# ScalarE's order within a tick: exponentials behind the copies and the side stages

## The chip, the core and the metric

The kernel runs on one core of a Trainium2 chip. The metric is the device time of the whole program in microseconds. It has five engines that matter here: TensorE (PE in the profile; PEld is its weight load), VectorE (DVE), ScalarE (ACT), GpSimd (POOL) and SyncE (SP), which only issues transfers here. Each runs its own list of instructions in order, and they wait for each other by semaphores.

## The reference, cut

Two layers over x of 16 sequences x 256 tokens x 128 features. All is float32.

```python
x  = L0_attn_x
xn = _layernorm(x)
s  = softmax attention of xn, 16 heads of 64, causal, then @ Wo + bo
g  = silu(top-1 routed experts(xn) + shared ffn(xn))
x  = x + s * g
xn = _layernorm(x)
s  = linear attention (elu + 1, cumulative sums, 16 heads of 8)
g  = silu(two transformer layers: l2-normed q and k, rotary,
          local attention with window 64, 8 heads of 64, gated gelu ffn)
x  = x + s * g
```

## The kernel before

The tokens are worked in 8 blocks `b` of 512 (4 tiles of 128 tokens, 2 sequences). The two softmax attentions (kind 0: the causal one of the first layer; kind 1: the local one, two layers `l` per block) are cut in the same way: a *pair* is two heads over both sequences of a block, a *step* is a pair over one sequence (`s` 0 or 1). There are 256 steps.

A plan written by hand (class `Plan`) lays the steps out over 348 *ticks*, at most one step in a tick; some ticks have none. It hangs everything else, the *side stages*, on ticks too: projections `qkv` of one tile of tokens, `lin` (the projections of the linear attention), `cum` (its cumulative sums as matmuls), `wo`, `glu`, `down1`, `v` (the values of kind 0, four banks), `ffn`, the experts `eT`, `eg`, `ed` of ticks 8 to 29, and so on. Every engine walks over the same ticks in its own function and writes its instructions in an order fixed by that function. So the order of an engine's work is the order of the lines in its tick loop, and nothing is moved at run time.

For the step `st` of tick t the work is spread over four ticks:

- TensorE in tick t: `logits` (L541, L544), each head into one of two `s` banks; in tick t+1: `transposes` of the weights `p` (L552), which wait for the exponentials; in tick t+2: `values` (L568, L571), and where s is 1 `merge` (L578), the transposes of the spread sums. Its own order in a tick is: `produce` (q or k of a coming pair, L521 or L531), `logits` of t, `transposes` of t-1, side stages of t, `values` and `merge` of t-2.
- VectorE in tick t: `masked` (L975) adds the mask, scales, takes the maximum; in tick t+1 `copies` of head 0 out of PSUM (L985), `inverse` of the sums (L991); in tick t+3 `scaled` (L996). Then its side stages: for `qkv` these are `mix` (L1158, L1162), `rot` (L1167), `rr` (inverse roots, from L1172) and `kn` (L1258).
- ScalarE in tick t: `exps` (L812, L813), four exponentials that wait for `masked`; in tick t+1 `copies` of head 1 (L826), which wait for `transposes`; in tick t+2 `merge` (L790, rT). `produce` (L790, q or k) evacuates a bank of q or k. Its side stages evacuate the banks that TensorE fills in the same tick: `qkv` five instructions (L889, L890 twice, L790), `lin` (L832, L833), `cum` (L840), `glu` (L911), `phi` (L895), `xT` (L877, L795, L796) and others.

All banks of q, k, merge and most side stages are one ring of two, `mm`. TensorE waits (`mm_bank`) until ScalarE has emptied the bank of two uses before. A `qkv` stage fills three of them, so its third bank waits for the first to be emptied. ScalarE's `raw` and `sq` buffers of a tile are double too, and `qkv` of a tile waits for `rot` of the tile two before (`rot_ready`).

GpSimd spreads the inverse sums (`expand`, L1272), rotates q and k of a tile (L1377, L1378), multiplies in `cum` (L1342) and whitens (L293). Every side stage of it waits for its input by semaphore.

A block has 36 ticks in the steady part. They hold, in this order: a run of four ticks with `qkv` of local layer 0 (ticks 111 to 114 for block 2), whose rotation ends in tick 115 and whose pairs are first produced in tick 116; then twelve `cum` ticks; `glu` of the layer before in tick 125; `glu` of this block in tick 135, in a stretch without steps; four `qkv` ticks of local layer 1 (138 to 141, steps only in the first two). Numbers of ticks below are of this block.

Of the kernel before, what the change touches and what calls it, by code (L numbers as in the profile page):

```python
# [781 lines left out]
def scalar(nc, act, c, plan, mm, s, pt, o):  # L782
# [19 lines left out]
    def produce(which, st):  # L802
        evacuate(c.qk[which][:, st.pair % 4, :], "qk"[which], st.pair)

    def exps(st):
        if st.s == 0 and st.pair >= 2:
            act.wait_ge(c.rden_ready, st.pair - 1)
        for h in range(2):
            u = 2 * st.n + h
            act.wait_ge(c.s_done, s.done("s", st.n, h))  # L810
            den, p = c.den[:, st.pair % 2, 2 * st.s + h, :], c.p[:, u % 4, :]
            A(p[:, 0:P], p[:, 0:P], ACT.Exp, bias=c.nmax[:, u % 4, 0:1], scale=-1.0, accum_out=den[:, 0:1])  # L812
            A(p[:, P:SB], p[:, P:SB], ACT.Exp, bias=c.nmax[:, u % 4, 1:2], scale=-1.0, accum_out=den[:, 1:2])\  # L813
                .then_inc(c.exp_done, 1)

    def merge(pair):
        if pair:
            act.wait_ge(c.o_done, o.done("o", pair - 1))
        evacuate(c.rT[:, :], "m", pair)

    def copies(st):
        u = 2 * st.n + 1
        act.wait_ge(c.pt_full, pt.full("t", st.n, 1))
        if st.n >= 2:
            act.wait_ge(c.pv_done, st.n - 1)
        A(c.pt[:, u % 4, :], c.pt_ps[pt.slot("t", st.n, 1)][:, 0:SB], ACT.Copy).then_inc(c.pt_done_act, 1)  # L826
# [104 lines left out]
    for tick in range(plan.length):  # L931
        for which, st in plan.produce.get(tick, ()):
            produce(which, st)
        if plan.step(tick):
            exps(plan.step(tick))
        if plan.step(tick - 1):
            copies(plan.step(tick - 1))
        if tick == 4:
            act.wait_ge(c.p1_loaded, c.P1_LOADS)
            act.wait_ge(c.hT_zero, 1)  # L940
        for seg in plan.side.get(tick, ()):
            if seg[0] in stage:
                stage[seg[0]](*seg[1:])
        if (st := plan.step(tick - 2)) and st.s == 1:
            merge(st.pair)

# [541 lines left out]
def program(nc, c, w, dram):  # L1488
    with ExitStack() as ctx:
        buffers(nc, ctx, c)  # L1490
        plan = Plan()
        rings = count_units(c, plan)
        c.CONST_LOADS = 16 * 8
        with nc.Block() as block:
            @block.sync
            def _(sp):
                sync(nc, sp, c, plan, *rings, dram, w)

            @block.tensor
            def _(pe):  # L1500
                tensor(nc, pe, c, plan, *rings)

            @block.scalar
            def _(act):
                scalar(nc, act, c, plan, *rings)

            @block.vector
            def _(dve):
                vector(nc, dve, c, plan, *rings)

            @block.gpsimd
            def _(pool):
                gpsimd(nc, pool, c, plan, *rings, dram)
# [81 lines left out]
```

## Time and profile before

| | us |
|---|---|
| median of three runs | 2309.12 (2306.81 to 2309.9) |
| the profiled execution | 2310.23 |
| its span | 2308.4 |
| TensorE busy | 1871.7 (81%) |
| VectorE busy | 1266.9 (55%) |
| ScalarE busy | 1239.2 (54%) |
| GpSimd busy | 805.3 (35%) |
| mean granted TensorE clock | 0.909 of full |

TensorE is the busiest engine and still idle for a fifth of the span, in pieces of 0.3 to 12 us. What the change does is to be read from those pieces: which engine ended them, and in which tick. Around the span lie 1.8 us of the profiled execution.

### The profile page before, as it was taken

To read this page: it belongs to the slowest core of one execution; us is meant where nothing else is said; L and a number is where in the kernel's file an instruction comes from. 1 tells how busy PE (TensorE), PEld (TensorE's weight loads), DVE (VectorE), ACT (ScalarE), POOL (GpSimd) and SP (SyncE) were. 2 spreads that over 40 slices of the span, in tenths; PEclk is the share of its full clock that TensorE was granted. 3 is DMA by queue.
4 is the path that set the end of the run, shared out by engine and by line. 5 is a ranking of instruction groups with operands and counts; after the bars stand their busy time and mean duration, and the time that the engine had idled before them with its cause. 6 is when DMAs were issued, how large, how long until landed. Compare 5 with 4: busy or idle time off the path is not lost.

```text
span 2308.4 us, 34655 instructions
## 1 busy us (share of the span) xinstructions
PE 1871.7 (81%) x10900; PEld 1169.5 (51%) x10900; DVE 1266.9 (55%) x4083; ACT 1239.2 (54%) x3559; POOL 805.3 (35%) x912
## 2 busy tenths in 40 slices
PE   5599987996789878887888779987888778857856
PEld 4377754554455445453555446544546345534534
DVE  4344446555655456546755565545655565466654
ACT  2445545654665546545565465555664566445534
POOL 2732224323432333214532343214432353244431
PEclk9799998997999989998999898988999899979978
DMA  7155400000000000000000000000000000000000
GB/s 226 37 175 168 157 17 8 1 1 6 1 1 14 6 1 1 15 1 1 6 1 15 1 1 1 19 1 1 1 10 6 1 1 1 5 5 1 6 0 5
DMA packets 49711, 53.26 MB, mean 23 GB/s; under 512 B 6386, under 2 KB 42236, under 8 KB 49532
## 3 DMA queue, kind: packets, MB, share of 16 engines
q0 software_dynamic: 7808, 27.79, 3.7%
q1 hardware_dynamic: 41724, 23.26, 3.5%
q8 instruction: 91, 1.49, 0.3%
q14 instruction: 88, 0.72, 0.1%
HBM read 41.60 MB, written 9.44 MB: 22 GB/s over the span
## 4 chain that ended last, share of the span: by engine, by line
PE 56%; DVE 15%; ACT 13%; issue 9%; POOL 6%; DMA 1%; DVEq 0%; SPq 0%; POOLq 0%; ACTq 0%
PE ps L596 5%; PE ps L568 5%; PE ps L552 4%; PE ps L521 4%; PE ps L544 4%; PE ps L541 4%; PE ps L670 3%; ACT p L812 3%; ACT p L813 3%; PE ps L531 3%; PE ps L578 2%; PE ps L512 2%; PE ps L679 2%; PE ps L725 2%; POOL h L293 2%
## 5 line engine op out<-in xcount | busy, mean ns | idle before, releaser
L812 ACT ACTIVATE p<-p,nmax 128x128 f32<-128x128 f32 x512 | 201.7, 394 | 359.8 <-DVE nmax L975 355.8
L975 DVE CUSTOM_DVE_ANT_0 p<-ps,mask,nrq 128x128 f32<-128x128 f32 (+1 forms) x512 | 183.0, 413 | 275.0 <-PE ps L544 275.0
L975 DVE CUSTOM_DVE_ANT_0 p<-ps,mask 128x128 f32<-128x128 f32 (+1 forms) x512 | 152.3, 354 | 263.7 <-PE ps L544 248.8
L670 PE MATMUL ps<-wqkv,hT 128*128 128x512 f32 x384 | 204.6, 643 | 99.3 <-ACT big L890 72.1
L1272 POOL COPY rdx<-rden 128x256 f32<-128x256 f32 x256 | 102.9, 431 | 521.0 <-DVE rden L991 520.1
L813 ACT ACTIVATE p<-p,nmax 128x256 f32<-128x256 f32 x512 | 252.3, 493 | 0.0
L552 PE MATMUL ps<-ident,p 128*128 128x128 f32 x1536 | 243.1, 296 | 5.8 <-ACT pt L826 2.0
L552 PEld LDWEIGHTS ps<-ident,p 128*128 128x128 f32 x1536 | 176.9, 149 | 101.1 <-issue 91.4
L531 PE MATMUL ps<-ident,big 128*128 128x128 f32 x512 | 92.9, 324 | 135.9 <-DVE big L1167 91.9
L1377 POOL TENSOR_TENSOR big<-big,rots 128x512 f32<-128x512 f32 x64 | 100.8, 1575 | 291.9 <-ACT big L890 291.7
L568 PE MATMUL ps<-pt,v 128*64 128x256 f32 x1024 | 178.9, 430 | 0.0
L544 PE MATMUL ps<-k,q 64*128 64x256 f32 x1024 | 170.5, 411 | 0.0
L670 PEld LDWEIGHTS ps<-wqkv,hT 128*128 128x128 f32 x384 | 64.6, 194 | 200.8 <-ACT big L890 124.8
L1342 POOL TENSOR_TENSOR big<-big,qkb 128x360 f32<-128x360 f32 (+1 forms) x96 | 82.4, 858 | 223.4 <-ACT big L840 222.9
L541 PEld LDWEIGHTS ps<-k,q 64*128 64x128 f32 x1024 | 85.1, 201 | 145.0 <-issue 81.0
L541 PE MATMUL ps<-k,q 64*128 64x128 f32 x1024 | 136.7, 346 | 25.5 <-DVE nmax L975 13.3
L985 DVE COPY pt<-ps 128x384 f32<-128x384 f32 x256 | 141.5, 553 | 22.0 <-PE ps L552 21.5
L531 PEld LDWEIGHTS ps<-ident,big 128*128 128x128 f32 x512 | 68.4, 165 | 161.7 <-issue 124.9
L790 ACT ACTIVATE rT<-ps 128x512 f32<-128x512 f32 x128 | 75.9, 593 | 134.9 <-PE ps L578 133.9
L596 PE MATMUL ps<-wo,attT 128*128 128x128 f32 x1024 | 134.8, 295 | 7.9 <-DVE attT L996 6.1
L596 PEld LDWEIGHTS ps<-wo,attT 128*128 128x128 f32 x1024 | 131.2, 210 | 16.6 <-issue 9.7
L790 ACT ACTIVATE q<-ps 128x512 f32<-128x512 f32 x128 | 76.1, 595 | 114.1 <-PE ps L531 76.9
(214 smaller groups left out, 4025.6 us busy)
## 6 DMA issues: line engine op xcount, KB each, us to landing
slots_in<-xn SPq DMA_DIRECT2D x1, 2560.0 KB, 14.0
v<-slots_in SPq DMA_DIRECT2D x20, 128.0 KB
slots_out<-v SPq DMA_DIRECT2D x20, 128.0 KB
big<-in_x SPq DMA_DIRECT2D x4, 512.0 KB, 6.3
x<-in_x SPq DMA_DIRECT2D x8, 256.0 KB, 3.0
out_x<-x SPq DMA_DIRECT2D x8, 256.0 KB, 2.3
wqkv<-in_wqkv SPq DMA_DIRECT2D x2, 768.0 KB
xn<-in_x SPq DMA_DIRECT2D x6, 256.0 KB, 3.3
```

Source lines behind the costliest of these rows:

```text
L531: last = nc.tensor.transpose(bank[:, t * P:(t + 1) * P], c.qkr[:, t, a:a + P], c.ident[:, :])
L541: MM(banks[h][:, 0:P], q[f:f + HD, 0:P], k[f:f + HD, 0:P], start=True, stop=True)
L544: MM(banks[h][:, P:SB], q[f:f + HD, P:SEQ], k[f:f + HD, :], start=True, stop=True).then_inc(c.s_full, 1)
L552: last = nc.tensor.transpose(bank[:, j * P:(j + 1) * P], c.p[:, u % 4, j * P:(j + 1) * P], c.ident[:, :])
L568: MM(bank[f:f + HD, q:q + SEQ], v[:, 2 * st.s, a:a + HD], pts[h][:, 0:SEQ], start=True, stop=False)
L596: last = MM(bank[:, t * P:(t + 1) * P], c.attT[kind][:, i, t * P:(t + 1) * P], w, start=i == 0, stop=i == LAST)
L670: MM(bank[:, :], c.hT[:, t * P:(t + 1) * P], c.wqkv[:, l, i * INNER1:(i + 1) * INNER1], start=True, stop=True).then_inc(c.mm_full, 1)
L790: A(dst, mm_bank(*name)[:, :], ACT.Copy).then_inc(c.mm_done, 1)
L812: A(p[:, 0:P], p[:, 0:P], ACT.Exp, bias=c.nmax[:, u % 4, 0:1], scale=-1.0, accum_out=den[:, 0:1])
L813: A(p[:, P:SB], p[:, P:SB], ACT.Exp, bias=c.nmax[:, u % 4, 1:2], scale=-1.0, accum_out=den[:, 1:2])\
L975: last = V.tensor_tensor_reduce(out=c.p[:, u % 4, a:b], in0=bank[:, a:b], in1=c.mask[st.kind][:, P * (1 - i):SEQ], scale=scale, scalar=3e3 ...
L985: V.tensor_copy(c.pt[:, u % 4, :], bank[:, 0:SB]).then_inc(c.pt_done, 1)
```

## The change

In ScalarE's tick loop the call of `exps` for the step of this tick moves from ahead of `copies` to behind the side stages. It still stands ahead of `merge` of the step two ticks before. No instruction is added or removed, and no other engine's order changes.

```diff
@@ scalar(), tick loop
         for which, st in plan.produce.get(tick, ()):
             produce(which, st)
-        if plan.step(tick):
-            exps(plan.step(tick))
         if plan.step(tick - 1):
             copies(plan.step(tick - 1))
...
         for seg in plan.side.get(tick, ()):
             if seg[0] in stage:
                 stage[seg[0]](*seg[1:])
+        if plan.step(tick):
+            exps(plan.step(tick))
         if (st := plan.step(tick - 2)) and st.s == 1:
             merge(st.pair)
```

ScalarE in a `qkv` tick of local layer 0 (tick 113), from the second head's exponentials or from the copy on. `p` are the weights, `pt` the transposed ones, `mn` belongs to `phi`, `big` holds `sq` and `raw`, `v1` the values of the local attention, ps0 and ps1 are the `mm` ring, ps5 is a bank of the transposes. Before:

```order
L812 ACTIVATE p,den<-p,nmax 128x128
L813 ACTIVATE p,den<-p,nmax 128x256
L826 ACTIVATE pt<-ps5 128x384
L895 ACTIVATE mn<-mn 128x256
L889 ACTIVATE big<-ps1 128x512
L890 ACTIVATE big<-ps1 128x512
L889 ACTIVATE big<-ps0 128x512
L890 ACTIVATE big<-ps0 128x512
L790 ACTIVATE v1<-ps1 128x512
```

and now:

```order
L826 ACTIVATE pt<-ps5 128x384
L895 ACTIVATE mn<-mn 128x256
L889 ACTIVATE big<-ps1 128x512
L890 ACTIVATE big<-ps1 128x512
L889 ACTIVATE big<-ps0 128x512
L890 ACTIVATE big<-ps0 128x512
L790 ACTIVATE v1<-ps1 128x512
L812 ACTIVATE p,den<-p,nmax 128x128
L813 ACTIVATE p,den<-p,nmax 128x256
```

The exponentials now stand behind the evacuation of all three banks of the projection.

ScalarE in the tick with four banks of values of kind 0 (tick 128; `v0` are those values, `big` with ps0 is the bank of a cumulative sum). Before:

```order
L813 ACTIVATE p,den<-p,nmax 128x256
L826 ACTIVATE pt<-ps5 128x384
L840 ACTIVATE big<-ps0 128x360
L790 ACTIVATE v0<-ps1 128x512
L790 ACTIVATE v0<-ps0 128x512
```

and now:

```order
L826 ACTIVATE pt<-ps5 128x384
L840 ACTIVATE big<-ps0 128x360
L790 ACTIVATE v0<-ps1 128x512
L790 ACTIVATE v0<-ps0 128x512
L790 ACTIVATE v0<-ps1 128x512
L790 ACTIVATE v0<-ps0 128x512
L812 ACTIVATE p,den<-p,nmax 128x128
L813 ACTIVATE p,den<-p,nmax 128x256
```

The evacuation of the cumulative sum, on which the second bank of values depends, has left its place behind the exponentials.

ScalarE in a `glu` tick with a step (tick 125; `ff` is the gated buffer). Now:

```order
L826 ACTIVATE pt<-ps5 128x384
L911 ACT_TABLE_LOAD
L911 ACTIVATE ff<-ps1,gb1 114x512
L911 ACTIVATE ff<-ps0,gb1 114x512
L911 ACTIVATE ff<-ps1,gb1 113x512
L840 ACTIVATE big<-ps0 128x360
L812 ACT_TABLE_LOAD
L812 ACTIVATE p,den<-p,nmax 128x128
```

The load of the exponential's table, which stood in the next tick, comes ahead of this tick's exponentials. The number of table loads is 32 in both programs.

## Rows read from the trace of the kernel before

**Rows 1.** Page, part 1: busy us, share of span, instructions.
```profile
PE 1871.7 (81%) x10900; PEld 1169.5 (51%) x10900; DVE 1266.9 (55%) x4083; ACT 1239.2 (54%) x3559; POOL 805.3 (35%) x912
```

**Rows 2.** Waits of TensorE: who, for whom, total us, times, longest us.
```profile
PE ps L531 <- DVE big L1167: 91.9, 15, 11.6
PE ps L506 <- POOL h L293: 78.3, 16, 7.8
PE ps L670 <- ACT big L890: 72.1, 48, 3.1
PE ps L670 <- ACT v L833: 26.8, 16, 3.1
...
PE ps L531 <- ACT v L833: 7.7, 9, 2.4
...
PE ps L521 <- ACT big L840: 6.1, 4, 2.5
PE ps L512 <- ACT big L840: 5.2, 3, 3.0
...
PE ps L552 <- ACT p L813: 1.1, 2, 0.8
```

**Rows 3.** Group by line and shape: count, busy us, mean ns, idle before.
```profile
L812 ACT ACTIVATE p<-p,nmax 128x128 f32<-128x128 f32 x512 | 201.7, 394 | 359.8 <-DVE nmax L975 355.8 <-issue 3.6
```

**Rows 4.** Windows: ticks 111 to 116; us, then busy of each engine, clock.
```profile
847.50:892.40 44.90, 33.04 (x178) 16.91 (x177) 32.30 (x81) 26.30 (x78) 22.35 (x24) 0.96 0.00 1
```

**Rows 5.** Timeline of tick 114: start us, length us, engine, line, idle before.
```profile
871.44 0.88 PE L552 MATMUL ps<-ident,p 128*128 128x128 f32 x6
872.15 1.88 PE L670 MATMUL ps<-wqkv,hT 128*128 128x512 f32 x4
...
873.47 0.40 ACT L812 ACTIVATE p<-p,nmax 128x128 f32<-128x128 f32 x1 [2.98 <-DVE nmax L975]
...
875.24 0.47 ACT L826 ACTIVATE pt<-ps 128x384 f32<-128x384 f32 x1
...
875.92 0.58 ACT L889 ACTIVATE big<-ps 128x512 f32<-128x512 f32 x1
...
877.03 1.12 PE L670 MATMUL ps<-wqkv,hT 128*128 128x512 f32 x2 [3.00 <-ACT big L890]
```

**Rows 6.** Timeline, end of the rotation of that run, ticks 114 to 116.
```profile
870.59 2.18 DVE L1167 TENSOR_TENSOR big<-big 128x1024 f32<-128x1024 f32 x1
...
878.89 2.17 DVE L1167 TENSOR_TENSOR big<-big 128x1024 f32<-128x1024 f32 x1
...
887.91 0.20 DVE L1172 TENSOR_SCALAR ss<-ss 128x64 f32<-128x64 f32 x1
...
892.39 1.09 PE L531 MATMUL ps<-ident,big 128*128 128x128 f32 x4 [3.80 <-DVE big L1167]
```

**Rows 7.** Timeline of a `cum` tick (122), transposes to transposes.
```profile
921.09 0.87 PE L552 MATMUL ps<-ident,p 128*128 128x128 f32 x6
...
921.80 0.77 PE L679 MATMUL ps<-big,tri 128*128 128x360 f32 x2
...
924.13 0.45 ACT L840 ACTIVATE big<-ps 128x360 f32<-128x360 f32 x1
...
924.74 0.88 PE L552 MATMUL ps<-ident,p 128*128 128x128 f32 x6
```

**Rows 8.** Timeline of tick 128, with four banks of values.
```profile
964.68 0.40 ACT L812 ACTIVATE p<-p,nmax 128x128 f32<-128x128 f32 x1 [2.48 <-DVE nmax L975]
...
967.32 4.34 PE L512 MATMUL ps<-wv,xnT 128*128 128x512 f32 x6 [3.03 <-ACT big L840]
```

**Rows 9.** Timeline of tick 125: table load and the wait of `glu`.
```profile
942.94 1.28 ACT L911 ACT_TABLE_LOAD   x1
...
944.24 1.27 ACT L911 ACTIVATE ff<-ps,gb 114x512 f32<-114x512 f32 x2
...
944.98 1.11 PE L716 MATMUL ps<-xT,g 128*113 128x512 f32 x2 [0.94 <-ACT ff L911]
```

## The prediction

> **What bounds the kernel now.** I read the busy shares first: TensorE works 1871.7 us of the 2308.4 us span, the next engine 1266.9 [rows 1]. So TensorE is the bound where it is busy, and the question is what ends its 437 us of idle time. The waits of TensorE answer that [rows 2]. Two large ones end with VectorE's last rotation (91.9 us, L531) and GpSimd's whitening (78.3 us, L506), at the end of long chains. The next two end with ScalarE emptying a bank for a projection: 72.1 and 26.8 us, 98.9 us in 64 waits, one per `qkv` tile, 1.5 us each. Smaller ones of the same make are 7.7 (`lin` bank) and 6.1 and 5.2 us (`cum` bank). The transposes, which need the exponentials, waited for them 1.1 us in all: the exponentials are early. The reader is to see in the groups that ScalarE stood idle 355.8 us ahead of L812, waiting for VectorE's masked logits [rows 3], while in its own queue behind them lay evacuations for which TensorE was waiting.
>
> Tick 114 shows it [rows 5]. TensorE has filled two banks of the projection from 872.15 on. ScalarE waits idle 2.98 us until 873.47 for the masks, does four exponentials, copies at 875.24, and starts on the first bank at 875.92. TensorE's third bank starts at 877.03 after 3.00 us of idleness.
>
> **The change, part by part.** It moves four exponentials (875.24 - 873.47 = 1.77 us from the first to the next instruction [rows 5], about 1.87 to the release of the transposes) behind the copy and the side stages. Nothing is added. Three things follow.
>
> (a) *The bank waits go.* I replayed ticks 111 to 116 with the durations of the rows: transposes 0.88, two banks 1.88, an evacuation of a q or k bank 1.1, the copy 0.47, exponentials 1.87, VectorE as in its rows. ScalarE empties the first bank as soon as it is full and `rot` of two tiles before is done. In tick 114 that is the end of L1167, 870.59 + 2.18 = 872.77 [rows 6]; the exponentials' place costs 3.1 us more. TensorE comes 0.5 us earlier in tick 111, 1.4 in 112, 2.1 in 113 and some 6 in 114 (of which up to 2 from the clock, which stood at half speed for a while behind that wait). In return the transposes now wait 0.5 to 1.2 us for exponentials in 111 to 113, which is in these numbers. But the run ends at VectorE's last rotation, and TensorE waits for it already, 3.80 us [rows 6]. VectorE is busy 32.30 of 44.90 us in the run [rows 4], and its idle time lies mostly ahead of tick 113. From there it is a full queue: masks, copies, mix, rotation. Its start into that queue moves up by 2.1 us (mix of the first tile), by 3.4 us at the third tile and 4.8 at the inverse roots (L1172, 887.91), as each tick's masks come earlier. I take 4.5 us for a run. The ends: nothing, if rotations beside a busy GpSimd (2.18 and 2.17 us here) eat it; 8 us, four waits at the mean of 1.5 us and 2 us of clock, if the chain shortens as much as TensorE. There are 8 runs: **-36 us** (0 to -64).
>
> Tick 128: the `cum` bank was emptied late because VectorE's `fin` delayed the masks [rows 8]. The wait of 3.03 us goes, and the exponentials still end ahead of the transposes, since three more banks of values stand between. Four such places hold most of 6.1 + 5.2 us [rows 2]: **-11 us** (-8 to -16). The `lin` waits [rows 2] are gone in the same way, 0.7 in each of 7 blocks: **-5 us** (-3 to -8). Local layer 1, tick 138: the wait there, the longest of L670's (3.1 us [rows 2]), goes, but the tick has no values and nothing to produce, so TensorE meets the transposes 3 us ahead of the exponentials. 0.3 us are left where no `wo` follows (4 of 6), 2.5 where one does: **-6 us** (0 to -19).
>
> (b) *The exponentials become late in short ticks.* What TensorE does between the last bank of the side stage and the next transposes is values (0.8), logits (0.86), sometimes merge (0.6) and produce (0.5 or 1.0). What ScalarE now does is evacuate (0.45 to 0.6) and exponentials 1.87, with 0.1 us of signalling twice. So ticks with a produce have cover, and others not. In tick 122 transposes follow transposes after 924.74 - 921.09 = 3.65 us, with a merge [rows 7]; the new chain is 0.71 + 0.77 + 0.1 + 0.45 + 1.87 = 3.90: 0.2 us lost. Where the merge is missing too (121, and 123, whose loss falls into the wait for the whitening that follows) it is 0.75. That is 0.9 in a block: **+7 us**. Ticks 118 and 119: merge's bank is emptied behind the exponentials, 0.35 us late, 7 times: **+2.5**. Ticks 127, 131 to 133: 0.1 to 0.2 each, eight blocks: **+5**. Tick 134 (`yT`, then no steps): 0.45, six times: **+2.7**. Ticks with `comb`, where ScalarE waits for the shared feed-forward first, five times 1 to 1.6, less what `xT` gains in the next tick: **+2**. The last eight steps have no side stages and run at 2.5 to 3.3 us a tick; copy and exponentials in a row need 3.3: **+2.5**. The first eight ticks: **+3**. Together **+25 us** (+12 to +60: if 0.2 us more is lost in each of some 150 steps without a produce behind them).
>
> Ticks 8 to 29 are filled by TensorE, and the exponentials had 5 us to spare: nothing, by 0.3 us and more of cover.
>
> (c) *The table load.* The load ahead of L812 moves one tick up, in front of exponentials that are now needed soon. The load takes 1.28 us [rows 9], and the gelus begin at the same time 0.94 us earlier for TensorE's third bank. By the replay 0.1 us is left: nothing. The Trainium skill, ScalarE: Activation LUTs, section What ACT_TABLE_LOAD costs, speaks against the change here: it puts a drain of about 1.38 us beside each load, 2.66 us for a switch. By that the eight `glu` ticks with a step would lose some 1.4 us more each and the sum would be about 11 us higher. In the trace the load runs from 942.94 and the first gelu starts at 944.24 [rows 9], 1.30 us later, so the row has no such drain and I go by the row.
>
> **The sum.** -36 - 11 - 5 - 6 + 25 = -33 us against the profiled execution's own 2310.2: 2277. The median lies 1.1 us below that execution, so **2276 us**.
>
> **The rivals.** First, *VectorE takes it back*: the runs are ended by the rotation, whatever ScalarE does. For it speaks that 91.9 us of TensorE's waits already end there [rows 2], and that rotations are slow when GpSimd works beside them. Against it, that VectorE had 12.6 us idle in the run [rows 4], each piece of it waiting for logits. Then the first term is -9 and the sum -6: 2303.
>
> Second, *the clock helps*. The mean granted clock of the run is 0.96 of full [rows 4]: 2 x 0.04 x 44.9 = 3.6 us at 1.2 instead of 2.4 GHz, one drop, and it stands behind the 3.00 us wait. If this and the like behind the other waits of 3 us stay away and none comes in their place, a drop of 3.4 us gives back 1.7, some 12 times: 2255. Against it: in tick 138 a wait of the same length stands in another place.
>
> Third, the other side, *the exponentials bind*: the new chain transposes, side bank, evacuation, exponentials, transposes becomes the beat of most ticks. It decides from 58 / 256 = 0.23 us lost per step, averaged over all steps. For it: all waits in (b) are new and the cover is a few tenths of a us in many ticks. In 150 steps without a produce behind them at 0.6 us it is 90 us against 58: 2341. Against it: the exponentials' mean wait today is nothing, and I counted the blocks' ticks one by one.
>
> **Chances.** Forecast 0.52 (2276, by itself 2259 to 2296); clock 0.16; VectorE 0.14; exponentials 0.16; other 0.02. A measurement can tell about 0.2% here, 4.6 us. Faster: 0.52 + 0.16 + half of VectorE's and a little = 0.77; same 0.07; slower 0.16. The range takes in the clock's case and VectorE's and leaves out most of the third: 2246 to 2312.
>
> **What would show it.** TensorE's L670 waits for ScalarE fall from 98.9 us to under 30; L552 waits for ACT p rise from 1.1 to 40 or more. The wait L531 for DVE L1167 stays near 90. ScalarE's idle time ahead of L812 falls well below 355.8, and idle time of L826 and L840 rises. The run of ticks 111 to 116 lasts 40.4 instead of 44.9 us. Ticks 122 and 123 are longer. If L552 waits over 90 us, the third rival holds and I was wrong in the cover; if the run keeps its length though L670's waits are gone, VectorE's.

## The result, and the profile after

| | before | after |
|---|---|---|
| median, us | 2309.2 (2306.81 to 2309.9) | 2232.35 (2230.72 to 2233.05) |
| ratio | | 0.9668 (0.9651 to 0.9685) |
| span of the profiled execution | 2308.4 | 2230.4 |
| TensorE busy | 1871.7 | 1856.1 |
| TensorE idle (span less busy) | 436.7 | 374.3 |
| mean granted clock | 0.909 | 0.914 |

The change takes 77 us away; the forecast was 33, and the time lies below the range. The direction was right, the size was not. Of the 78 us between the two spans, 62.4 are idle time of TensorE and 15.6 are busy time: the same 10900 instructions, run at a better clock. I keep the two apart in all that follows. They are not independent: time that TensorE wins by the clock it can lose again by waiting longer for an engine that it now reaches earlier.

Page of after, part 1 (answers to [rows 1]):

```profile
PE 1856.1 (83%) x10900; PEld 1157.0 (52%) x10900; DVE 1273.5 (57%) x4083; ACT 1248.0 (56%) x3559; POOL 785.9 (35%) x912
```

Waits of TensorE after (answers to [rows 2]): who, for whom, total us, times, longest us.

```profile
PE ps L531 <- DVE big L1167: 94.4, 15, 10.6
PE ps L506 <- POOL h L293: 73.0, 16, 7.8
PE ps L552 <- ACT p L813: 47.3, 95, 2.2
PE ps L670 <- ACT big L890: 27.3, 56, 2.8
...
PE ps L531 <- ACT hT L796: 8.0, 7, 1.3
```

L670's waits for ScalarE were 72.1 and 26.8 us in two rows; one of 27.3 is left. `lin` (7.7) and `cum` (6.1 and 5.2) are gone from the list. In their place stands L552 for ACT p, 47.3 us in 95 waits. The two long chains ahead of it hardly moved.

Groups by line and shape after (the first answers to [rows 3]): busy us, mean ns, idle ahead of it. ScalarE's wait for the masks fell from 355.8 to 66.8 us; what it waits for now is TensorE's transposes.

```profile
L812 ACT ACTIVATE p<-p,nmax 128x128 f32<-128x128 f32 x512 | 200.4, 391 | 67.1 <-DVE nmax L975 66.8
L826 ACT ACTIVATE pt<-ps 128x384 f32<-128x384 f32 x256 | 125.7, 491 | 175.6 <-PE ps L552 175.6
```

The run of ticks 111 to 116, from its first logits to the bank filled from the last rotation (answers to [rows 4], same columns), and out of its timeline ticks 113 and 114 (to [rows 5, 6]):

```profile
813.30:852.70 39.40, 32.02 (x178) 16.12 (x178) 33.06 (x83) 28.04 (x84) 20.63 (x23) 0.98 0.01 1
```

```profile
833.75 0.52 PE L552 MATMUL ps<-ident,p 128*128 128x128 f32 x3
834.30 0.19 ACT L813 ACTIVATION_READ_ACCUMULATOR p<-p,nmax 128x1 f32 x1
834.63 0.52 PE L552 MATMUL ps<-ident,p 128*128 128x128 f32 x3 [0.36 <-ACT p L813]
834.99 1.88 PE L670 MATMUL ps<-wqkv,hT 128*128 128x512 f32 x4
...
836.57 0.60 ACT L889 ACTIVATE big<-ps 128x512 f32<-128x512 f32 x1 [0.59 <-DVE big L1167]
...
837.71 1.12 PE L670 MATMUL ps<-wqkv,hT 128*128 128x512 f32 x2 [0.84 <-ACT big L890]
...
851.29 1.22 DVE L1167 TENSOR_TENSOR big<-big 128x1024 f32<-128x1024 f32 x1
852.65 1.08 PE L531 MATMUL ps<-ident,big 128*128 128x128 f32 x4 [4.69 <-DVE big L1167]
```

The run lasts 39.4 instead of 44.9 us (forecast 40.4). ScalarE waits 0.59 us for a rotation and then empties the first bank; TensorE's wait of 3.00 us is 0.84. The run still ends with the rotation, and TensorE waits 4.69 us for it instead of 3.80. The first rows hold what the forecast got wrong: **head 0's transposes start at 833.75, while head 1's exponentials run until 834.5**. Only head 1 waits, 0.36 us, and a good part of ScalarE's time is covered by TensorE's work on head 0.

**Where the 78 us lie.** For each of the 256 steps I took the time from one start of transposes to the next in both traces, with TensorE's busy time in it, and grouped the steps by the side stages of their tick:

| ticks with | steps | idle, us | busy, us | the forecast's term |
|---|---|---|---|---|
| `qkv` of layer 0, and the end of its run | 47 | -33.0 | -9.1 | -36 |
| `xT` or `lin` | 20 | -12.1 | -3.2 | -5 |
| `v`, or the tick behind `fin` | 15 | -11.6 | -7.8 | -11 |
| `qkv` of layer 1, and the end of its run | 18 | -3.3 | +2.4 | -6 |
| `cum` alone, and all others | 156 | -2.6 | +2.4 | +25 |
| sum | 256 | -62.5 | -15.2 | -33 |

The forecast's terms are times, with a little of the clock in the first, so idle and busy together are their fair counterpart: -42, -15, -19, -1 and nothing (-0.2) against -36, -5, -11, -6 and +25. The clock's part of the gain lies where waits of 3 us went. TensorE's busy time at half speed (granted clock 0.50) fell from 52 to 24 us in the first row and from 12.6 to nothing in the third; in the whole program it fell from 296 to 252 us.

### The profile page after: what moved, and what is told of

Its sections match the earlier page's. It is cut to its first block, busy times and chain, and to the rows that moved or that the text cites. A ratio compares the mean times of both kernels' runs of the same rounds, so it can differ in the third digit from the quotient of the medians.

```text
span 2230.4 us, 34655 instructions
## 1 busy us (share of the span) xinstructions
PE 1856.1 (83%) x10900; PEld 1157.0 (52%) x10900; DVE 1273.5 (57%) x4083; ACT 1248.0 (56%) x3559; POOL 785.9 (35%) x912
## 4 chain that ended last, share of the span: by engine, by line
PE 60%; DVE 15%; ACT 9%; issue 8%; POOL 6%; DMA 1%; DVEq 0%; SPq 0%; POOLq 0%; ACTq 0%
PE ps L552 6%; PE ps L596 5%; PE ps L670 5%; PE ps L568 4%; PE ps L521 4%; PE ps L544 3%; PE ps L541 3%; PE ps L578 3%; PE ps L679 3%; ACT p L813 3%; DVE big L1162 2%; PE ps L512 2%; PE ps L531 2%; POOL h L293 2%; PE ps L725 2%
## 5 line engine op out<-in xcount | busy, mean ns | idle before, releaser
L552 PE MATMUL ps<-ident,p 128*128 128x128 f32 x1536 | 250.4, 294 | 48.1 <-ACT p L813 47.3
L1272 POOL COPY rdx<-rden 128x256 f32<-128x256 f32 x256 | 94.7, 399 | 554.6 <-DVE rden L991 554.6
L552 PEld LDWEIGHTS ps<-ident,p 128*128 128x128 f32 x1536 | 172.8, 147 | 156.6 <-issue 153.1
L812 ACT ACTIVATE p<-p,nmax 128x128 f32<-128x128 f32 x512 | 200.4, 391 | 67.1 <-DVE nmax L975 66.8
L670 PE MATMUL ps<-wqkv,hT 128*128 128x512 f32 x384 | 208.1, 658 | 27.7 <-ACT big L890 27.3
L826 ACT ACTIVATE pt<-ps 128x384 f32<-128x384 f32 x256 | 125.7, 491 | 175.6 <-PE ps L552 175.6
L531 PE MATMUL ps<-ident,big 128*128 128x128 f32 x512 | 92.2, 325 | 124.7 <-DVE big L1167 94.4
L1377 POOL TENSOR_TENSOR big<-big,rots 128x512 f32<-128x512 f32 x64 | 87.9, 1374 | 274.7 <-ACT big L890 268.2
L544 PE MATMUL ps<-k,q 64*128 64x256 f32 x1024 | 165.7, 400 | 0.0
L531 PEld LDWEIGHTS ps<-ident,big 128*128 128x128 f32 x512 | 69.3, 166 | 148.0 <-issue 126.3
L670 PEld LDWEIGHTS ps<-wqkv,hT 128*128 128x128 f32 x384 | 67.9, 202 | 134.3 <-ACT big L890 84.7
L596 PE MATMUL ps<-wo,attT 128*128 128x128 f32 x1024 | 130.2, 289 | 7.9 <-DVE attT L996 6.1
L596 PEld LDWEIGHTS ps<-wo,attT 128*128 128x128 f32 x1024 | 126.5, 204 | 15.3 <-issue 8.5
## 6 DMA issues: line engine op xcount, KB each, us to landing
slots_in<-xn SPq DMA_DIRECT2D x1, 2560.0 KB, 14.6
```

Source lines behind the costliest of these rows:

```text
L531: last = nc.tensor.transpose(bank[:, t * P:(t + 1) * P], c.qkr[:, t, a:a + P], c.ident[:, :])
L544: MM(banks[h][:, P:SB], q[f:f + HD, P:SEQ], k[f:f + HD, :], start=True, stop=True).then_inc(c.s_full, 1)
L552: last = nc.tensor.transpose(bank[:, j * P:(j + 1) * P], c.p[:, u % 4, j * P:(j + 1) * P], c.ident[:, :])
L596: last = MM(bank[:, t * P:(t + 1) * P], c.attT[kind][:, i, t * P:(t + 1) * P], w, start=i == 0, stop=i == LAST)
L670: MM(bank[:, :], c.hT[:, t * P:(t + 1) * P], c.wqkv[:, l, i * INNER1:(i + 1) * INNER1], start=True, stop=True).then_inc(c.mm_full, 1)
```

## The experiments

Each ratio is against the kernel before, timed beside the run on the same chip; its medians there were 2308.4 to 2309.2 us. Busy and idle time (span less TensorE's busy time) are those of the one profiled execution.

| kernel | median | ratio (95%) | TensorE busy | idle |
|---|---|---|---|---|
| before | 2309.2 | | 1871.7 | 436.7 |
| changed | 2232.4 | 0.9668 (0.9651 to 0.9685) | 1856.1 | 374.3 |
| a2 changed, again | 2232.8 | 0.9675 (0.966 to 0.969) | 1855.1 | 375.1 |
| e1 layer 0's `qkv` ticks only | 2268.0 | 0.9818 (0.9798 to 0.9837) | 1862.0 | 405.0 |
| e2 all but layer 1's `qkv` ticks | 2235.5 | 0.9686 (0.967 to 0.9703) | 1851.3 | 379.8 |
| e3 ticks without `qkv` only | 2274.3 | 0.9852 (0.9836 to 0.9869) | 1857.6 | 416.6 |
| e4 transposes wait for both heads | 2245.1 | 0.9728 (0.9711 to 0.9744) | 1829.9 | 412.9 |
| e5 exponentials behind the copy only | 2312.0 | 1.0016 (1.0007 to 1.0025) | 1866.9 | 442.1 |
| e7 ticks of the forecast's losses only | 2286.8 | 0.9905 (0.989 to 0.992) | 1853.2 | 431.6 |
| e8 waits filled, two kinds | 2321.3 | 1.0056 (1.0042 to 1.0069) | 1903.4 | 416.1 |
| e9 layer 1: exponentials between two banks | 2210.1 | 0.9575 (0.9561 to 0.959) | 1836.1 | 371.6 |
| e10 `xT` and `lin` ticks only | 2291.0 | 0.9924 (0.9909 to 0.9939) | 1862.8 | 427.3 |
| e11 waits filled, runs only | 2309.2 | 1.0001 (0.9992 to 1.001) | 1886.4 | 421.9 |
| e12 changed, 1.85 us of work put in | 2235.4 | 0.9688 (0.9673 to 0.9702) | 1856.2 | 376.4 |

**The theory** after the comparison: the bank waits go as forecast, the losses don't come, because head 0's transposes run beside head 1's exponentials, and the clock adds the rest. **The rivals**: the forecast's prices are right and something else won 45 us; it is the earlier copy that wins; it is all the clock.

### Parts of the change, one at a time (e1, e3, e7, e10)

In each the exponentials stand last only in some ticks. For e1:

```diff
+    def late(tick):
+        layers = {seg[2] for seg in plan.side.get(tick, ()) if seg[0] == "qkv"}
+        return 0 in layers
...
+        if plan.step(tick) and not late(tick):
+            exps(plan.step(tick))
         if plan.step(tick - 1):
             copies(plan.step(tick - 1))
...
-        if plan.step(tick):
+        if plan.step(tick) and late(tick):
             exps(plan.step(tick))
```

In e3 the condition is `not layers`; in e7 it is that the tick's stages hold none of `qkv`, `xT`, `lin`, `v` and those of the tick ahead no `fin`; in e10 that they hold `xT` or `lin` and no `qkv`. In e2, below, it is `1 not in layers`.

> Exponentials last only in the ticks that hold `qkv` of local layer 0 (the eight runs, ticks 111 to 114 and their like); everywhere else as in the kernel before. Theory A (the two traces lie side by side and the shifts add): the runs alone give their -43 us, 2266 (2258 to 2274). Rival B, the prediction's own sizes: -36, 2273. Rival C (the rest of the change only gives back what the runs win): below 2240.

> Exponentials last only in the ticks without any `qkv` stage (cumulative sums, values, xT, lin, glu and the rest). Theory A (the per-tick comparison of the two traces): -37 us, 2272 (2264 to 2280). Rival B, the prediction's terms for these ticks, -11 - 5 + 25: +9, 2318. The sum of this and of the run with only the `qkv` ticks of layer 0 tells too whether the parts add.

The two came out at 2268 and 2274, -41 and -34 us: -75 together, where e2, which has both parts, has -73 and the changed kernel -77. The times of the parts add; idle time alone adds less well (-31.7 and -20.1 against -56.9 in e2), and the clock makes up for it. In e3 theory A holds (2272) and the forecast's terms (+9, 2318) don't. e1 lies in theory A's range, 2258 to 2274, but that range holds rival B's 2273 too, and its single executions spread from 2261 to 2269: it can't tell the two apart. It does refute rival C.

> Exponentials last only in ticks that have no `qkv`, `xT`, `lin` or `v` stage and no `fin` in the tick ahead: the 177 steps in which nothing was to be won and the prediction put its losses. The prediction's terms: +25, 2334 (2321 to 2369). Theory A, from the traces (+4.6 us in these ticks, of which some is clock): 2312 (2308 to 2318).

Measured 2287: below both. The idle time fell by 5.1 us; the forecast put 25 us of losses here. Part of the gain is the neighbours'. `fin` stands in one of these ticks (127), and with the exponentials behind the side stages ScalarE does its part of it (L918) sooner. VectorE's `fin` no longer waits for that, so the masks of tick 128 and the bank behind them come earlier: TensorE's wait there is 1.93 instead of 3.03 us [rows 8], and the transposes start 2.5 us earlier. Before, then e7 (where VectorE's lines have moved by six):

```profile
961.33 0.69 DVE L1200 SCALAR_TENSOR_TENSOR h<-h,xb 128x512 f32<-128x512 f32 x1 [1.19 <-ACT h L918]
```

```profile
951.72 0.87 DVE L1206 SCALAR_TENSOR_TENSOR h<-h,xb 128x512 f32<-128x512 f32 x1
...
957.88 2.94 PE L512 MATMUL ps<-wv,xnT 128*128 128x512 f32 x6 [1.93 <-ACT big L840]
```

In the 156 steps of the table's last row idle time fell by 3.9 us and busy time rose by 1.7. The greater part of the gain, 18.5 us, is busy time, and it lies in other ticks: -5.3 in those with `v` or behind `fin`, -9.3 in layer 1's, -4.2 in those with `xT` or `lin`. Why the clock is better in the last two is not shown.

> Exponentials last only in the ticks with `xT` or `lin` and no `qkv` (20 steps). Theory A (the trace after: besides the `lin` waits of 0.7 the wait of L531 for ACT hT L796, 4.5 us in tick 108, shrinks to 1.3; the prediction had left that row out): TensorE's idle time -10 us (-8 to -13), with what the clock adds 2294 (2286 to 2300). Rival B, the prediction's term: -5, 2304.

Measured 2291, idle -9.4, busy -8.9: theory A. The forecast counted `lin` alone. The longer wait in the same place, tick 108, was in the view of TensorE's waits of before, and I passed over it:

```profile
PE ps L531 <- ACT hT L796: 13.6, 7, 4.5
```

Timeline of tick 108 before, and below it after:

```profile
834.56 0.59 ACT L796 ACTIVATE hT<-ps 64x510 f32<-64x510 f32 x1
...
835.21 1.11 PE L531 MATMUL ps<-ident,big 128*128 128x128 f32 x4 [4.53 <-ACT hT L796]
```

```profile
803.37 0.59 ACT L796 ACTIVATE hT<-ps 64x510 f32<-64x510 f32 x1
...
804.02 0.66 PE L531 MATMUL ps<-ident,big 128*128 128x128 f32 x4 [1.29 <-ACT hT L796]
```

The bank of q waits for the one that `xT` filled, which three evacuations empty; they stood behind the exponentials.

### The copy alone (e5)

```diff
         if plan.step(tick - 1):
             copies(plan.step(tick - 1))
+        if plan.step(tick):
+            exps(plan.step(tick))
...
-        if plan.step(tick):
-            exps(plan.step(tick))
```

> Of the change only the half that moves the exponentials behind the copy; they stay ahead of the side stages. Theory A (the banks are what counts): the bank waits stay and are 0.5 us longer in places where the copy used to stand behind idle exponentials: within 5 us of the kernel before, 2309. Rival B (the earlier copy of the transposed weights brings the values and the rest of the tick forward): 2290 or less.

Measured 2312, 1.0016 (1.0007 to 1.0025). L670 still waits 72.3 and 26.1 us. The gain comes from the side stages' place; the copy's alone is worth nothing (idle +5.4, busy -4.8).

### Both heads (e4)

```diff
-            pe.wait_ge(c.exp_done, u + 1)
+            pe.wait_ge(c.exp_done, 2 * st.n + 2)
```

> The changed kernel, with one wait made stricter: the transposes of head 0 wait for the exponentials of both heads, not of their own. Theory A (the prediction's replay charged all four exponentials to the transposes, while TensorE really starts when head 0's two are done; this is why its +25 us of losses did not come): 111 steps start their transposes less than 0.1 us after the last exponential, 68 us in sum, of which head 1's own wait of 0.36 in some 60 steps is saved: +30 us (15 to 47), 2262. Rival B (the cover was there anyway, the heads do not matter): within 5 us of 2232.

TensorE's waits, e4:

```profile
PE ps L552 <- ACT p L813: 94.3, 108, 3.1
```

The wait doubles, by 47.0 us, and the idle time grows by 38.6. Step by step it is what the theory says: in tick 121 the transposes take 0.81 us more to come, in 123 0.84, and part of it comes back in the next tick (0.26 in 122) since head 1 waits no more. The total grew by 12.7 us only, just under the lower end of what I expected, because TensorE was busy 26.2 us less.

So the price of the heads' overlap has to be read by place. In the 156 steps of the last row idle time grows by 17.0 us and busy time falls by 14.6: +2.4 in all. Where the forecast had put losses the steps do become longer, over all blocks 10.2 us in ticks 121 to 123, 5.8 in 132 and 133, 2.4 in the last eight. The steps behind them give it back, 13.6 in tick 124, 5.5 in 126, 4.4 in 134. In tick 124 TensorE waits for the whitening of h by GpSimd (L506), whatever came ahead of it, and this wait is now 2.75 instead of 3.28 us. Behind the longer one the granted clock falls, behind the shorter one it doesn't. The window from there to the next transposes, changed kernel, then e4; us, busy of each engine, clock:

```profile
893.60:901.00 7.40, 7.31 (x31) 4.02 (x31) 0.92 (x1) 4.19 (x12) 1.65 (x2) 0.65 0.00 0
```

```profile
899.90:904.80 4.90, 4.85 (x30) 2.77 (x30) 0.92 (x1) 3.75 (x12) 1.61 (x2) 1.00 0.00 0
```

The mechanism is shown, by the places that became longer; what it is worth in the whole can't be read from the median.

### Layer 1 (e2, e9)

> As the changed kernel, but in the ticks with `qkv` of local layer 1 (138, 139 and their like) the exponentials stand ahead again. Theory A (there the third bank's wait was only exchanged for 2.2 and 1.7 us of waiting ahead of the transposes): 2230, within 5 us of the changed kernel. Rival B, the prediction's -6 for this place is real: 2238. Rival C (the exchange lengthens the rotation chain behind it): 2222.

Measured 2235.5, 3 us above the changed kernel, and the intervals overlap: between theory A and rival B it can't decide. Idle time is 5.5 us more than in the changed kernel, about what the forecast gave this part (-6), and busy time (-4.8) takes most of it back. After, tick 138 and 139:

```profile
988.71 1.13 PE L670 MATMUL ps<-wqkv,hT 128*128 128x512 f32 x2 [0.40 <-ACT big L890]
...
992.92 0.52 PE L552 MATMUL ps<-ident,p 128*128 128x128 f32 x3 [2.22 <-ACT p L813]
993.79 0.52 PE L552 MATMUL ps<-ident,p 128*128 128x128 f32 x3 [0.36 <-ACT p L813]
...
1000.23 0.52 PE L552 MATMUL ps<-ident,p 128*128 128x128 f32 x3 [1.65 <-ACT p L813]
```

Here the exponentials truly bind: 22 of the 47 us of L552's waits stand in the twelve ticks of this kind. So e9 puts them between the evacuations of the first and the second bank, which TensorE's third bank doesn't need:

```diff
         for i in range(2):
+            if l and i and plan.step(tick):
+                exps(plan.step(tick))
             bank = mm_bank("qkv", b, l, t, i)
...
-        if plan.step(tick):
+        if plan.step(tick) and not any(seg[0] == "qkv" and seg[2] for seg in plan.side.get(tick, ())):
             exps(plan.step(tick))
```

> The changed kernel, but in the ticks with `qkv` of local layer 1 the exponentials stand between the evacuation of the first bank and that of the second. Theory A (the third bank needs only the first one emptied, so both waits shorten: L552's of 2.2 and 1.7 us by 1.1 to 1.7 each in six blocks): -6 to -16 us against the changed kernel, 2222. Rival B (the exponentials' masks or the next tick's banks are late, or the rotation chain ends these ticks anyway): 2232 within 5 us.

The same place in e9:

```profile
989.76 1.13 PE L670 MATMUL ps<-wqkv,hT 128*128 128x512 f32 x2 [0.40 <-ACT big L892]
...
992.15 0.52 PE L552 MATMUL ps<-ident,p 128*128 128x128 f32 x3 [0.41 <-ACT p L813]
...
997.28 0.52 PE L552 MATMUL ps<-ident,p 128*128 128x128 f32 x3
```

Measured 2210.1, the fastest of all and 22 us below the changed kernel. The waits shorten as expected (2.22 to 0.41, 1.65 to nothing), -13.9 us in these ticks, but 7.3 come back as a longer wait for the rotation, as rival B said, and over the whole program the idle time falls by only 2.7. The other 20 us are busy time, 10.0 of them in layer 1's ticks, where the waits were shortened, and 7.9 in the `xT` and `lin` ticks behind them; busy time at half speed fell from 252 to 205 us. So this is a gain by the clock, not by the waits as such.

### The clock (e8, e11, a2, e12)

> The kernel before, order and waits unchanged, but TensorE repeats a matmul inside two kinds of its 3 us waits for ScalarE, ahead of the signal: the second bank of the last `qkv` tile of local layer 0 (four times in place of once), and the cumulative sum in the tick behind `fin` (four or eight times). The results are the same. Theory A (idleness of TensorE brings the granted clock to 0.50 behind such a wait, as after tick 114 at 878.21 and in tick 128 at 966.96; that is the 1.7 us by which tick 128 won more than its wait of 3.03): about 12 stretches of 3.4 us at half speed stay away, -20 us, 2289 (2282 to 2302), with L670's and L512's waits shorter by just the added work. Rival B (the clock does not depend on these waits, or the stretches only move elsewhere): within 5 us of 2309, and the mean granted clock stays at 0.909.

The cumulative sum was overfilled: in tick 128 sixteen instructions took 5.01 us where a wait of 3.03 stood, and other ticks behind `fin` have less to fill. At 2321 it fits neither 2289 nor 2309 within 5 us, and says nothing on the total. It was repeated without that part:

```diff
         for i in range(3):
             bank = mm_bank("qkv", b, l, t, i)
-            MM(bank[:, :], c.hT[:, t * P:(t + 1) * P], c.wqkv[:, l, i * INNER1:(i + 1) * INNER1],
-               start=True, stop=True).then_inc(c.mm_full, 1)
+            for _ in range(4 if (l, t, i) == (0, 3, 1) else 1):
+                last = MM(bank[:, :], c.hT[:, t * P:(t + 1) * P], c.wqkv[:, l, i * INNER1:(i + 1) * INNER1],
+                          start=True, stop=True)
+            last.then_inc(c.mm_full, 1)
```

> The kernel before with its order and waits; TensorE runs the second bank's matmul of the last `qkv` tile of local layer 0 four times in place of once, ahead of the signal, so eight of its 3 us waits are filled with work of the same length (3 x 0.92 us). The results are the same. The run with the cumulative sums filled too had added about 5 us of work where the wait was shorter. Theory A (the idleness brings the half-speed stretch behind the wait, as at 878.21): idle -20, time at half speed shorter by 20 to 35 us, and the whole 2300 (2295 to 2304). Rival B (no link between wait and clock): 2309 within 4 us, with the half-speed stretches where they were.

Windows behind the filled wait of tick 114, the same instructions; us, busy of each engine, clock. Before, then e11:

```profile
877.00:882.80 5.80, 5.77 (x24) 2.78 (x24) 4.00 (x3) 2.75 (x5) 4.16 (x2) 0.71 0.01 3
```

```profile
877.00:881.20 4.20, 4.18 (x25) 2.02 (x25) 4.00 (x3) 2.73 (x5) 3.19 (x2) 1.00 0.01 4
```

In this place theory A holds: with the wait filled the clock stays at 2.4 GHz, and the next transposes start 1.64 us earlier; so too in ticks 78 (1.57), 222 (1.58) and 294 (1.53). The expectation was wrong about the other four. Three of those waits were 1.5 to 1.8 us long, with at most 0.8 us of work at half speed behind them in their step, and the work put in was longer than they were; the fifth wait of 3.00 us (tick 258) had no drop of the clock behind it in the kernel before. So such a wait brought a stretch at half speed in four of five places, and filling it took the stretch away in all four. Only 6.3 us could be won in this way, not 20.

In the whole rival B holds: 1.0001. The three overfilled waits cost 1.6 us, and the rest comes back within the block, 0.70 in tick 117, 0.30 in 124, 1.18 in 144: -4.5 us in the runs, +4.3 in all other ticks. TensorE's time at half speed fell from 420 to 413 us (granted clock 0.909 and 0.911), less than the 14 us of these four stretches.

> The changed kernel once more, unedited, to see how much of TensorE's busy time is the clock's chance. Theory A (the half-speed stretches belong to the waits of the kernel): busy within 3 us of 1856.1, idle within 2 us of 374.3. Rival B (they lie differently in each execution): busy off by 5 us or more, idle the same.

> The changed kernel with 1.85 us of repeated matmuls in tick 52 (first bank of the values of block 2, half 1, three times in place of once; the results are the same), so that everything behind it lies 1.85 us later and nothing else changes. Theory A (the half-speed stretches follow the waits): +1.9 us, busy time +2 to +4. Rival B (where a wait lies against the clock's own steps decides whether it costs a stretch): busy time off by 6 to 25 us in either direction with the same idle time.

Busy 1855.1 and 1856.2, medians +0.5 and +3.1 us. In e12 the added work shows as 1.7 us of busy time in its own tick; elsewhere busy time is 1.6 us less and idle time 2.1 more. Still theory A both times: most of the stretches belong to the kernel and stay with its work when all of it is moved by 1.85 us. The kernel before has one profile, and its single executions lie between 2303.8 and 2310.8 us, with granted clocks of 0.912 to 0.908: the profiled one (2310.2) is among the slow ones, so some us of the 15.6 can be its own. And that the rest belongs to the change is not to say that the waits which went explain all of it.

## Why the prediction was right or wrong

**The bank waits (a).** Right in mechanism and, for the runs, in size: -33.0 idle and -9.1 busy against -36 in all, 39.4 us a run against 40.4, the rotation as the limit. L670's waits fell to 27.3 (under 30 was foretold), L531's for L1167 stayed at 94.4. `v` and the tick behind `fin`: -11.6 idle against -11, and -7.8 busy besides. Layer 1: -3.3 idle against -6, and -0.9 with the busy time. **Mis-sized**: `xT` and `lin` at -5 where they gave -12.1 (-15.3 with the busy time); the `hT` wait of 4.5 us was not in the sum.

**The losses (b).** This is the step that failed: +25 forecast; measured -2.6 idle and +2.4 busy in the changed kernel, and in e7, which changes nothing else, -5.1 idle over the whole program. The replay let the transposes wait for "four exponentials (875.24 - 873.47 = 1.77 us ..., about 1.87 to the release of the transposes)". The release that head 0 needs comes half-way. Tick 121 was to lose 0.75 and lost nothing, tick 122 0.2 and lost 0.46, tick 123 nothing. After, from the transposes of tick 121's step to those of 122's:

```profile
881.00 0.55 PE L552 MATMUL ps<-ident,p 128*128 128x128 f32 x3
881.08 0.49 ACT L813 ACTIVATE p<-p,nmax 128x256 f32<-128x256 f32 x1
...
881.81 0.52 PE L552 MATMUL ps<-ident,p 128*128 128x128 f32 x3 [0.26 <-ACT p L813]
...
885.11 0.88 PE L552 MATMUL ps<-ident,p 128*128 128x128 f32 x6
```

In the runs the replay had transposes wait 0.5 to 1.2 us in ticks 111 to 113; they wait 0.36, 0 and 0.36. Ticks 121 to 123 became 4.1 us longer over all blocks. With both heads bound (e4) they are another 10.2 longer: 14.3, where the forecast's 0.75, 0.2 and 0.75 a block make 13.6. So the replay had the price right for a wait that isn't there, and e4 puts this wait in. (The forecast counted +7, since it let tick 123's loss fall into the wait for the whitening behind it, and in e4 tick 124 does give it back.) The same holds for ticks 132 and 133 (nothing, and 5.8 in e4, against +5 with 127 and 131) and the last eight steps (+0.9, and 3.3 in e4, against +2.5). The other terms fell away for their own reasons, which I only looked up and didn't test: ticks 118 and 119 (+0.4 against +2.5), the ticks with `yT` (-0.1 against +2.7) and the first eight (within 0.4 us of nothing each, +0.1 together, against +3) had their cover, and tick 127 became 2.8 us shorter over all blocks.

The sign named for this step, "L552 waits for ACT p rise from 1.1 to 40 or more", came true (47.3) and proved nothing: 22 us are layer 1's, 18 are waits of head 1 of up to 0.36 us, and 7 are waits of head 0, of up to 1.29 us, in 17 places. In the short ticks these replaced other idle time or came back behind them. A wait's sum was the wrong witness; idle and busy time by tick are the right one.

**The table load (c).** Right. After, tick 125:

```profile
908.74 1.28 ACT L812 ACT_TABLE_LOAD   x1
...
910.03 0.40 ACT L812 ACTIVATE p<-p,nmax 128x128 f32<-128x128 f32 x1
...
911.16 0.41 PE L552 MATMUL ps<-ident,p 128*128 128x128 f32 x2 [0.24 <-ACT p L813]
```

The first exponential starts 1.29 us after the load starts, so no drain stands between; the Trainium skill (ScalarE: Activation LUTs, What ACT_TABLE_LOAD costs) has one of 1.38 us beside each load, and the measurement decides. The wait behind it is 0.24 and 0.36 us. This step is 0.90 us shorter than before and that of tick 124 0.89 longer: nothing, as forecast.

**The clock.** The sum had it at nothing beside the runs; it was a rival at 0.16 with about 20 us. Measured: 15.6. As a mechanism the rival is right where waits of 3 us went: busy time fell by 9.1 us in the runs and 7.8 in the ticks with `v` or behind `fin`. Tick 128 gained 4.70 us for a wait of 3.03: its six matmuls of values took 4.34 us [rows 8] at a granted clock that was 0.50 from 966.96 on, and run at full speed after. But e11 shows that such gains need not add up in the whole, e7, e9 and e4 have clock gains of 18 to 26 us in other places, and that these cancelled here (+2.4, +2.4 and -3.2 in the other rows) is not explained. That its number came near is in part luck.

**The balance**, in idle and busy time together: -33 forecast; losses 25 less, `xT` and `lin` 10 more, `v` and `fin` 8 more, the runs 6 more, layer 1 5 less: -77. The third rival (exponentials bind) and VectorE's are refuted by the table. The range failed because its lower end took in the clock's case alone: the losses that don't come and the clock lie on the same side, and it has no room for both.

## What to carry to other kernels

A consumer may need only the first part of what it waits for: replay each wait at the grain of its semaphore (here a head), not of the step. List every wait that the moved work ends, from the view of waits, before summing; and split a measured gain into idle and busy time, by place, since the second part can be the clock's and may not follow from the waits that went. An engine that serves two consumers should first empty what frees the other's next step, and do its own long work between two such pieces where the other has none (e9: the waits shortened by 13.9 us in their ticks, though most of the 22 us in the whole came by the clock).

## What the runs showed of the hardware

- With the same 10900 instructions TensorE's busy time was 1871.7 us at a mean granted clock of 0.909 (before) and 1829.9 at 0.924 (e4). In two profiled executions of the changed kernel it was 1856.1 and 1855.1. The kernel before varied more: 2303.8 to 2310.8 us, at 0.912 to 0.908.
- Behind five waits of 3.00 us the granted clock was 0.50 for some 3.4 us in four places and stayed at 1.00 in the fifth. With the waits filled with matmuls it stayed at 1.00 in all five, and the time of the program was where it was (1.0001).
- A wait of 3.28 us in tick 124 had a stretch of 0.50 behind it, and one of 2.75 us in the same place (e4) had none. One pair doesn't make a rule.
- In the two kernels e4 and e9 small changes of order or waits gave 26 and 20 us of busy time. What decides it stays open.
